# Two-layer graph attention on one core: the maximum is spread in mid first tile; in the stages without elu the exponentials stand ahead of the division, tiles are turned sooner, hT is copied ahead of the row's sort

## The reference

```python
h = jnp.maximum(_layernorm(x), 0.0)
Wh = h @ W;  e = (Wh @ a1)[:, :, None] + (Wh @ a2)[:, None, :]
e = jnp.where(e > 0, e, 0.2 * e)
att = softmax(jnp.where(adj > 0, e, -big), axis=-1)
x = x + elu(att @ Wh)        # layer 0
x = x + att @ Wh             # layer 1: the same with its own W, a; no elu
```

## Time and profile before

| | us |
|---|---|
| median of three runs (lowest, highest) | 293.23 (292.43, 293.95) |
| the profiled execution | 292.44 |
| its span, first to last instruction | 290.6 |
| PE busy | 285.6 (98%) |
| DVE busy | 257.2 (88%) |
| ACT busy | 191.9 (66%) |
| POOL busy | 82.4 (28%) |

### The profile page before, as it was taken

One profiled execution on the slowest core, in us unless ns is written; L12 is line 12 of the kernel. 1 busy time (PEld: TensorE's weight loads), 2 busy tenths in 40 slices (PEclk: granted clock), 3 DMA queues, 4 the chain that ended last, 5 costly groups with the idle time before them and its releaser, 6 DMA issues.

```text
span 290.6 us, 6680 instructions
## 1 busy us (share of the span) xinstructions
PE 285.6 (98%) x2527; PEld 283.9 (98%) x2527; DVE 257.2 (88%) x524; ACT 191.9 (66%) x496; POOL 82.4 (28%) x159
## 2 busy tenths in 40 slices
PE   7999999999999999999999999999999999999996
PEld 6999999999999999999999999999999999999996
DVE  4798899898999989899998989889797988599986
ACT  3386876794968869595885958477485747653500
POOL 2712703307061340705225070512407042000000
PEclk9999999999999999999999999999999999999999
DMA  7999959589595968859495884969969598796712
GB/s 226 416 407 406 406 144 409 234 331 408 173 416 206 379 246 339 330 180 413 145 388 222 309 359 169 362 240 352 363 241 366 204 338 344 257 380 223 267 72 74
DMA packets 26412, 85.32 MB, mean 294 GB/s; under 512 B 4990, under 2 KB 6156, under 8 KB 26380
## 3 DMA queue, kind: packets, MB, share of 16 engines
q1 hardware_dynamic: 25804, 84.50, 76.6%
q10 hardware_dynamic: 576, 0.39, 0.5%
HBM read 80.62 MB, written 4.26 MB: 292 GB/s over the span
## 4 chain that ended last, share of the span: by engine, by line
PE 93%; DMA 3%; issue 2%; DVE 1%; ACT 1%
PE acc L996 72%; PE prj L924 9%; PE tp L861 5%; PE acc L1011 2%; DMA in_row<-row_mem 1%; DMA row_mem<-sqr 1%; ACT row_r L466 1%; PE prj L896 1%; PE tp L943 1%; PE prj L1011 1%; PE prj L996 1%; PE acc L905 1%; PE tp L937 1%; PE tp L949 0%; PE tp L957 0%
## 5 line engine op out<-in xcount | busy, mean ns | idle before, releaser
L996 PE MATMUL acc<-wh,pbuf 128*128 128x129 f32 x1968 | 227.8, 275 | 0.7 <-DVE accs L746 0.5
L996 PEld LDWEIGHTS acc<-wh,pbuf 128*128 128x128 f32 x1968 | 224.0, 192 | 1.2 <-issue 0.9
L720 DVE SCALAR_TENSOR_TENSOR pbuf<-row_r,sqr,adj_sb 128x1024 f32<-128x1024 f32 x125 | 155.2, 1278 | 4.1 <-ACT row_r L466 4.0
L481 ACT ACTIVATE accs<-accs,rec 128x128 f32<-128x128 f32 x120 | 36.7, 389 | 42.7 <-DVE rec L756 42.7
L309 POOL TENSOR_TENSOR mean<-stats 128x8 f32<-128x8 f32 x14 | 13.5, 967 | 139.7 <-DVE stats L607 138.5
L413 ACT ACTIVATE xn<-x_sb,shift,rstd 128x128 f32<-128x128 f32 x120 | 47.7, 480 | 0.0
L466 ACT ACTIVATE row_r<-in_row 128x1024 f32<-128x1024 f32 x14 | 29.5, 2111 | 11.0 <-DMA in_row<-row_mem 10.9
L438 ACT ACTIVATE wh<-prj,wh 128x128 f32<-128x128 f32 x120 | 32.9, 367 | 0.0
L924 PE MATMUL prj<-w_ext,hT 128*128 128x130 f32 x240 | 29.3, 275 | 0.0
L924 PEld LDWEIGHTS prj<-w_ext,hT 128*128 128x128 f32 x240 | 28.0, 191 | 0.0
L338 POOL TENSOR_TENSOR rstd<-vareps,neg_half 128x8 f32<-128x8 f32 x15 | 26.0, 1732 | 6.8 <-DVE vareps L626 5.7
(11 more groups left out here) (109 smaller groups left out, 174.4 us busy)
## 6 DMA issues: line engine op xcount, KB each, us to landing
adj_sb<-in_adj SPq DMA_DIRECT2D x128, 512.0 KB, 9.0
in_row<-row_mem SPq DMA_DIRECT2D x13, 641.0 KB, 4.1
x_sb<-in_x SPq DMA_DIRECT2D x7, 512.0 KB, 8.5
out_x<-x_sb SPq DMA_DIRECT2D x7, 512.0 KB, 9.8
in_row<-row_mem SPq DMA_DIRECT2D x1, 512.0 KB, 4.4
x_sb<-in_x SPq DMA_DIRECT2D x1, 256.0 KB, 3.4
x_sb<-in_x ACTq DMA_DIRECT2D x1, 256.0 KB, 3.6
row_mem<-sqr SPq DMA_DIRECT2D x14, 4.0 KB
```

The lines of the kernel that those rows point to most:

```text
L481: op = nc.scalar.activation(hp[:, t, :], hp[:, t, :], ACT.Copy, scale=rec[:, t:t + 1])
L720: nc.vector.scalar_tensor_tensor(pbuf[:, t, :], row_r[:, n % 2, :], sqr[:, n % 2, 0, t:t + 1], adj_at(n, t), ALU.max, ALU.min).then_inc(p_ ...
L996: mm = nc.tensor.matmul(sum_at(k, s), pbuf[:, t, i * P:(i + 1) * P], wh[:, n % 2, t, :], start=(t == 0 and s == 0 and k < NB), stop=(t == ...
```

## The change

```diff
--- ACT, iteration n
                 if n == LAST:
                     seed_last()
-                scale_accs(n - 1)
-                if n < LAST:
+                if n < LAST and not elu:
                     if n % 2 == 0:
                         copy_u(n)
                     exps(n + 1)
+                scale_accs(n - 1)
+                if n < LAST:
                     if elu:
+                        if n % 2 == 0:
+                            copy_u(n)
+                        exps(n + 1)
                         elu_exp(n - 1)
                     if n + 2 <= LAST:
                         normalise(n + 2)
-                    early = T // 2 if elu else T
-                    scale_wh(n + 1, range(early))
-                    sort_row(n + 1)
-                    if early < T:
-                        scale_wh(n + 1, range(early, T))
+                    if elu:
+                        scale_wh(n + 1, range(T // 2))
+                        sort_row(n + 1)
+                        scale_wh(n + 1, range(T // 2, T))
+                    else:
+                        scale_wh(n + 1)
                 if n + 2 <= LAST:
                     copy_hT(n + 2)
+                if n < LAST and not elu:
+                    sort_row(n + 1)
--- DVE, iteration n
                 copy_e(n + 1)
-                masks(n, (DRAIN,))
-                exp_args(n + 1)
+                if l == 0:
+                    masks(n, (DRAIN,))
+                    exp_args(n + 1)
+                else:
+                    exp_args(n + 1)
+                    masks(n, (DRAIN,))
--- PE
-            def attend(n, tiles):
+            def attend(n, tiles, emax_of=None):
...
+                        if t == 0 and i == T // 2 and emax_of is not None:
+                            spread_emax(emax_of)
...
-                attend(n, (0,))
-                spread_emax(n + 1)
-                attend(n, (1, 2, 3, 4, 5))
+                k = 6 if stages[n - 1][0] == 0 else 4
+                attend(n, (0,), emax_of=n + 1)
+                attend(n, range(1, k))
                 if n + 2 <= LAST:
                     transposes(n + 2)
-                attend(n, (6, 7))
+                attend(n, range(k, T))
```

## The result

The changed kernel takes 296.75 us (median of 6 runs, 296.59 to 296.87); the kernel before took 293.62 in the same comparison (292.43 to 294.28). The ratio is 1.0103, 95% interval 1.007 to 1.0136: slower by 1.0%, 3.1 us. The forecast was 297.7, slower. The profiled execution took 296.82 us for a span of 295.0; before it was 292.44 for 290.6. Between the two traces the difference is 4.4 us, and 4.45 were forecast.

The account below looks back on a forecast made before the run. PE, working without a gap in mid kernel, was taken as the bound. Five waits of 1.03 us (5.15) less 0.7 at the seam gave 4.45 us on 293.23, so 297.7 us, own range 296.4 to 298.8.

Parts of the forecast that it names:

- PE as the bound, no gain in mid kernel: Iterations 1 to 13: PE works without a gap, so reordering DVE and ACT gains nothing there.
- The spread in mid tile at nothing: PE asks for the spread 0.893 us sooner, 0.16 us after the maximum is there; costs nothing.
- Arguments ahead of mask 2 at nothing: Without elu, mask 2 ends at 209.97, 0.29 us before PE wants it for tile 2; costs nothing.
- rival B: Beside the transposes' stall, spread and mask 2 make PE wait and the seam gives nothing: 300.0 us, chance 0.10.
- Steps 1 to 6: Iterations 9 to 13: division behind exponentials delays `xn`, tiles turn sooner; PE stands 1.03 us each at the transposes, 5.15 us.
- Rival C: PE's wait gives ACT time, so the stall at the transposes shrinks to perhaps half: 295.1 us, chance 0.06.
- hT ahead of the sort at nothing: ACT's sort behind hT makes DVE's copy of the sums 0.3 us late, but PE asks 1.5 us on; costs nothing.
- rival A: No stall: PE never waits for `xn`, only the seam's 0.7 us is won: 292.5 us, chance 0.06.
- The seam: From iteration 14 to 15, the row comes 0.89 us sooner and PE's wait goes; gain 0.7 us, between 0 and 0.7.

Follow-up runs that it names:

- e4: Kernel before with only the spread moved into mid first tile: 292.72 us, ratio 0.9974 to the kernel before.
- e1: Changed kernel with the tiles turned behind tile 5 again in all iterations: 299.03 us, ratio 1.0185 to the kernel before.
- e3: Changed kernel with ACT's division put back ahead of the exponentials, tiles still turned behind tile 3: 292.27 us, ratio 0.9974 to the kernel before.
- e10: Changed kernel with four of eight division instructions put back ahead of the exponentials in iterations without elu: 292.08 us, ratio 0.9944 to the kernel before.
- e2: Changed kernel with the tiles turned behind tile 4, one tile later: 292.0 us, ratio 0.9953 to the kernel before.
- e5: Changed kernel with the tiles turned behind tile 2, one tile sooner: 308.85 us (two runs, 307.23 and 310.48).
- e7: Kernel before with only hT put ahead of the row's sort, in iterations without elu: 297.21 us, ratio 1.011 to the kernel before.
- e6: Changed kernel with the tiles turned behind tile 5 and the row sorted ahead of hT again: 292.55 us, ratio 0.9963 to the kernel before.
- e9: Kernel before with the store of stage 12's graph issued after the last row's load: 292.54 us, ratio 0.9972 to the kernel before.

## Why the prediction was right, point by point

- **PE as the bound, no gain in mid kernel:** held. Iterations 1 to 8 take the same time as before, and no profiled execution of any version came below a span of 290.1 (the shortest unprofiled ones lie at 289.9).
- **The spread in mid tile at nothing:** held in the changed kernel, where no row is late. Its 0.16 us of room is gone when one is: in e4 the spread waited 0.27 us in iteration 14. In e1, where the sums came late, the maximum was late too, as a consequence, and that cost 0.31 us in each of five iterations.
- **Arguments ahead of mask 2 at nothing:** held, no wait at tile 2 (rival B did not occur).
- **Steps 1 to 6:** `xn` was whole 216.86 - 209.53 = 7.33 us behind the spread, 7.34 by the steps; the wait was 1.04 against 1.03, five times. Of it 0.06 comes back right behind, so the term is 4.9 and not 5.15. e3 and e10 take the division out of the way and the wait goes, e2 moves the ask and it goes, e5 moves it the other way and it grows by a tile. Rival C, that the wait is partly absorbed, is refuted by e5.
- **Weight loads at the wait:** in iteration 11 the first transposes' load started at 216.93, 0.07 us after `xn` was whole, and its matmul 0.03 us behind it. The wait for `xn` stands ahead of the load in PE's program, and none of the eight loads began before it had ended.
- **hT ahead of the sort at nothing:** right for the changed kernel, where the sort ended at 221.84 and the masks and the copy (224.36) stayed ahead: the first bank is copied 2 us before the next tile 0 asks. But rival A was worked out as if only `xn` mattered. With tiles turned late this edit costs 4.9 us by itself (e7). The prediction named the room it leaves only in terms of a late row, and missed that a late transpose does the same. Had the transposes stayed where they were, its term of nothing would have been wrong by 4.9 us.
- **The seam:** mechanism right, size off, and this is where the forecast difference of 4.45 and the measured 3.1 part. In the two profiles the gain is what was forecast, 0.7. Against the runs it is more: the term was taken from one of the best of the kernel before's executions. Its median lies 1.2 above its first profiled execution, while the changed kernel's median is that of its profiled one. 4.9 of waits less the 3.1 measured leaves about 1.8 us for what the kernel before loses to late rows. Its first profile shows 0.7 of that and its second 1.4; that the rest is of the same kind is inferred from the spread of the runs.
- **What the prediction did not see:** PE's wait is not a pure loss. The writes of the rows stay at 1.4 us in the changed kernel, so it pays for no late row, neither at the seam nor before it. The prediction let the row come 0.89 us sooner by the exponentials alone and took its write's time as given; in iteration 14 that write fell from 3.35 to 1.41 us.
- **Where it was lucky:** the two profiles' 4.4 us match the 4.45 because the kernel before's profiled execution was one of its faster ones, and because 0.25 too much in the waits is offset in part by the 0.1 us longer start. The absolute time, 296.75, lies within the forecast's own range of 296.4 to 298.8 because the kernel before was measured at 293.62 and not at 293.23; the difference, 3.13, is just under the 3.17 with which that range begins (296.4 - 293.23).

The versions without the five waits beat both kernels: e2 (292.0) and e10 (292.08) by 0.5% of the kernel before, e3, e6, e9 and e4 by 0.3 to 0.4%. e2 and e10 keep all edits of the change, with the tiles turned one tile later, or half of the division taken back in front.

## What to carry to other kernels

When the bounding engine has no idle, read for each operand it will ask for how long before the ask it is whole, and sum an edit's two effects, a later operand and an earlier ask, against that one number: here 4.06 us of room, 3.57 spent by the earlier ask and 1.47 by the reordered producer. A piece that stands early in an engine's order but behind a waiting one is late (in e1 ACT's sort, its row landed, stood behind hT, which waited 1.76 us): whether "hT before the sort" gains or costs was decided by where another engine had put the transposes. A term that rests on a DMA's landing is to be sized by the spread of the runs, not by one profile. And where DMAs only just keep pace, as in the table above, ask what a wait of the bounding engine gives back to them: here 4.9 us of waits cost 3.1.

## What the runs showed of the hardware

- The same 4 KB write to DRAM took 1.40 to 4.99 us to the issue of its read back, within iterations 9 to 14 of the traces above. SP issues it, among 128 adj transfers of 512 KB, into the queue q1, which moved 84.50 of the 85.32 MB of the run before. In the kernel before it grew from 1.42 to 3.45 us over iterations 9 to 13; in the changed kernel, whose iterations are 0.98 us longer, it stayed at 1.40 to 1.52.
- TensorE's granted clock was 1.00 through and behind five waits of 1.04 us (changed kernel) and fell to 0.50 of full speed at three of five waits of 2.58 us (e5), which cost 4.8 us on top of the waits in one execution; the other lost 1.5 us. Before each of the five PE had worked without a gap since the wait before, so what told the three from the two is not settled by these runs. Only one trace holds such a fall.
